# Three waits at stage boundaries removed, and 8 to 14 unread identity products on TensorE at the end of four stages

## The reference, cut to what matters

```python
x = x + jnp.tanh(g_xattn[0]) * _L0_xattn_ref(_layernorm(x), ctx, ctx, Wq, bq, Wk, bk, Wv, bv, interference, amp, Wo, bo)
x = x + jnp.tanh(g_ffn[0])   * _L0_ffn_ref(_layernorm(x), W, bias, A, Bf, coeffs, scales)       # dense + low rank
x = x + jnp.tanh(g_xattn[1]) * _L1_xattn_ref(_layernorm(x), ctx, Wq, bq, Wk, bk, Wv, bv, Wo, bo) # window of 16 keys
x = x + jnp.tanh(g_ffn[1])   * _L1_ffn_ref(_layernorm(x), weight, bias, centroids, assignments)  # clusters select
```

## Time and profile before

| | |
|---|---|
| three runs | 2049.05, 2052.22, 2054.82 us (median 2052.22) |
| the profiled execution's own time | 2051.24 us |
| its span, first to last instruction | 2049.1 us |
| PE busy | 1948.1 us, 95% of the span |
| mean granted TensorE clock | 0.980 |
| DVE, ACT, POOL busy | 52%, 33%, 18% |
| DMA | 328.62 MB, mean 160 GB/s |

### The profile page before, as it was taken

One profiled execution on the slowest core, in us unless ns is written; L12 is line 12 of the kernel. 1 busy time (PEld: TensorE's weight loads), 2 busy tenths in 40 slices (PEclk: granted clock), 3 DMA queues, 4 the chain that ended last, 5 costly groups with the idle time before them and its releaser, 6 DMA issues. The chain is left out here.

```text
span 2049.1 us, 50169 instructions
## 1 busy us (share of the span) xinstructions
PE 1948.1 (95%) x20126; PEld 1582.2 (77%) x20126; DVE 1072.4 (52%) x1868; ACT 681.4 (33%) x1152; POOL 360.1 (18%) x332
## 2 busy tenths in 40 slices
PE   7999889999997999999999899999689999999999
PEld 7999889999996777777777477777467777777887
DVE  5444241112114555555555465555578888874445
ACT  2222231111102344444434211111156666665121
POOL 0000000000001111111101210000256666651000
PEclk9999999999997899999999999999799999999999
DMA  5332335433348545544543434544664444433434
GB/s 200 124 123 103 145 106 184 169 122 137 116 163 300 204 167 215 203 174 190 226 185 115 161 113 185 184 184 164 198 188 149 140 131 142 148 113 114 150 134 147
DMA packets 149431, 328.62 MB, mean 160 GB/s; under 512 B 56433, under 2 KB 82673, under 8 KB 141105
## 3 DMA queue, kind: packets, MB, share of 16 engines
q1 hardware_dynamic: 147344, 326.04, 44.5%
q10 hardware_dynamic: 1952, 0.60, 0.1%
HBM read 200.25 MB, written 125.83 MB: 159 GB/s over the span
## 5 line engine op out<-in xcount | busy, mean ns | idle before, releaser
L1191 ACT ACTIVATE a_pt<-a_st_bank 128x1024 f32<-128x1024 f32 x128 | 131.3, 1026 | 266.3 <-PE a_st_bank L1239 266.3
L1528 POOL TENSOR_TENSOR a_sm<-a_sm,a_nmax 113x1024 f32<-113x1024 f32 x84 | 159.7, 1908 | 89.2 <-DVE a_nmax L1581 89.2
L1137 DVE TENSOR_REDUCE a_nmax<-a_s_bank 128x8 f32<-128x1024 f32 x124 | 151.7, 1223 | 20.6 <-PE a_s_bank L1227 14.0
L226 PE MATMUL q_qb<-q_xt_hi,wq_hi 128*128 128x256 f32 x512 | 146.2, 286 | 2.8 <-DVE wq_lo L168 2.8
L226 PE MATMUL kv_banks<-kv_ct_hi,wk_hi 128*128 128x256 f32 x512 | 146.0, 285 | 2.9 <-DVE wk_lo L168 2.9
L226 PE MATMUL kv_banks<-kv_ct_hi,wk_lo 128*128 128x256 f32 x512 | 145.5, 284 | 0.0
L226 PE MATMUL q_qb<-q_xt_lo,wq_hi 128*128 128x256 f32 x512 | 145.4, 284 | 0.0
L226 PE MATMUL q_qb<-q_xt_hi,wq_lo 128*128 128x256 f32 x512 | 145.4, 284 | 0.0
L226 PE MATMUL kv_banks<-kv_ct_lo,wk_hi 128*128 128x256 f32 x512 | 145.4, 284 | 0.0
L1821 PE MATMUL a_s_bank<-a_ks,a_qs 64*49 64x256 f32 x1344 | 95.5, 399 | 24.4 <-DMA a_ks<-k 11.8
L1575 DVE TENSOR_TENSOR a_sm<-a_s_bank,a_band 113x1024 f32<-113x1024 f32 x84 | 102.6, 1222 | 21.4 <-PE a_s_bank L1821 18.2
(11 more groups left out here) (228 smaller groups left out, 4595.2 us busy)
## 6 DMA issues: line engine op xcount, KB each, us to landing
k<-raw SPq DMA_DIRECT2D x32, 512.0 KB, 4.6
a_qs<-q SPq DMA_DIRECT2D x16, 1024.0 KB, 5.2
a_ks<-k SPq DMA_DIRECT2D x16, 1024.0 KB, 7.1
a_vraw<-v SPq DMA_DIRECT2D x32, 304.0 KB
q_xin<-in_x SPq DMA_DIRECT2D x16, 512.0 KB, 5.6
q<-q_out_lo SPq DMA_DIRECT2D x16, 512.0 KB, 4.1
q<-q_out_hi SPq DMA_DIRECT2D x16, 512.0 KB, 4.8
kv_cin<-in_ctxT SPq DMA_DIRECT2D x8, 1024.0 KB, 5.5
```

Of the source, the lines that this page charges most:

```text
L226: m = pe.matmul(out, a(x, c), b(y, c), start=(i + j == 0), stop=(len(terms) * j + i == n - 1))
L1137: dve.tensor_reduce(to, scores[:].rearrange("p b (h x) -> p b h x", h=4), X, ALU.max, negate=True).then_inc(maxed, 1)
L1191: act.activation(pt[:, s % 2], st_bank[:].rearrange("p b (h x) -> p (b h) x", h=4), ACT.Exp).then_inc(expd, 1)
L1528: pool.tensor_tensor(sm[live, k], sm[live, k], nmax[live, k, :].unsqueeze(2).to_broadcast([LIVE, 16, KEYS]), ALU.add).then_inc(shifted, 1)
```

## The change

Four parts, all at the boundaries.

1. A helper `keep_clock` multiplies the identity by itself n times into a PSUM tile that nobody reads: 14 products at the end of project_q, project_kv and ffn0_project1, 8 at the end of attention0. In project_kv PE waits first for the last key output (`klo`).
2. project_kv no longer loads `a_k_second`; `k_second` is no tile of its own any more, and attention0 loads the keys of slot 1 itself, as its third DMA.
3. In attention0 the loads of slot 2 wait for nothing new. Those of slot 3 now wait until ACT has written the first row of maxima (`rowed`).
4. The first queries and keys of layer 1 and the mask are loaded in the last turn of ffn0_project1, into SBUF that the low-rank factors have left. POOL zeroes that place in ffn0_project1, so half of the zeroing at the start of attend1_select_ffn1 falls away. The feed-forward weights' high part `f1_hi` is split over two places to make room.

```diff
+def keep_clock(pe, e, bank, n):
+    for _ in range(n):
+        pe.matmul(bank, e.ident[:], e.ident[:], start=True, stop=True)
...
@@ project_q, PE, end
+            keep_clock(pe, e, tb[:, 0, 0:P], 14)
...
@@ project_kv, SP
-            def last_keys(s):
-                if s == 1:
-                    sp.wait_ge(k_out, 160 * G + START)
-                    unit_keys(1)
...
-            staggered(sp, G, 2, [(2, load), (None, first_units), (None, output_weights), (0, store_k), (None, last_keys), (0, store_v)],
+            staggered(sp, G, 2, [(2, load), (None, first_units), (None, output_weights), (0, store_k), (0, store_v)],
...
@@ project_kv, PE, end
+            pe.wait_ge(klo, done(NC * G - 1))
+            keep_clock(pe, e, kb[:, 0, 0:P], 14)
...
@@ ffn0_project1, SP
+            def first_operands(s):
+                if s == 1:
+                    sp.wait_ge(e.op_zero, 2)
+                    for j in range(2):
+                        sp.wait_ge(qk_out[j][0], 16 + START)
+                    sp.dma_start(e.qs_first[:, 0:D], e.q1[0]).then_inc(e.op_in, 16)
+                    for c in range(4):
+                        sp.dma_start(e.ks_first[c:P:4, c, PADL:PADL + D], e.k1[0][c:P:4, :]).then_inc(e.op_in, 16)
+                    sp.dma_start(e.band[:], e.i["band"]).then_inc(e.op_in, 16)
+
+            steps = [(None, first_operands), (4, load_x), (1, load_ctx), (0, store_qk(1, e.k1)), (1, store_x2),
...
@@ ffn0_project1, POOL, after the first three roots
+            pool.wait_ge(w.lr, NC)
+            pool.memset(e.ks_first[:], 0.0).then_inc(e.op_zero, 1)
+            pool.memset(e.qs_first[:, D:DPAD], 0.0).then_inc(e.op_zero, 1)
...
@@ attention0, SP
+            sp.wait_ge(e.k_out, 160 * (B // 2 - 1) + START)
...
-                if s % G or filling(u):
+                if s % G or filling(u) and u == 0:
                     return
...
-                if isinstance(u, int) and u == NU:
-                    sp.wait_ge(shift_in[0], 16)
+                if isinstance(u, int) and u == NU + G:
+                    sp.wait_ge(rowed, 1)
                 sp.wait_ge(st_done, done(u - 13))
...
@@ attention0, PE, end
+            keep_clock(pe, e, s_bank[:, 0, 0:P], 8)
...
@@ attend1_select_ffn1
-            sp.wait_ge(pads[0], 2)
...
+                    if isinstance(t, int) and t == 0:
+                        continue
...
-                if s == -16:
-                    sp.dma_start(band[:], e.i["band"]).then_inc(const, 16)
...
-            pool.memset(ks[:, 0, 2:4], 0.0).then_inc(pads[0], 1)
-            pool.memset(qs[:, :, D:DPAD], 0.0).then_inc(pads[3], 1)
+            pool.memset(qs1[:, D:DPAD], 0.0).then_inc(pads[3], 1)
...
-            dve.memset(ks[:, 0, 0:2], 0.0).then_inc(pads[0], 1)
```

More of the change, by code:

```diff
@@ L46 @@
 DPAD = 1048
+HOLD = 5312
 NCL = 64
@@ L751, in ffn0_project1 @@
         sb, ps, sem = scope(nc, ctx)
+        sb("f0_hold", [P, HOLD - 4 * D])
         ln1 = Norm(nc, ctx, "fln"); ln2 = Norm(nc, ctx, "pln")
@@ L771, in ffn0_project1 @@
         qk_out = [[later(e, nc, f"p1_{c}_out{k}") for k in range(2)] for c in "qk"]
+        e.op_zero = later(e, nc, "a_op_zero"); e.op_in = later(e, nc, "a_op_in")
         e.f0_out = [*x_out, *v_out, *qk_out[0], *qk_out[1]]
@@ L1003, in attention0 @@
         qs = e.q_first + [sb(f"a0_qs{k}", [P, pairs, P], F32R) for k in range(2, 4)]
-        ks = e.k_first + [sb(f"a0_ks{k}", [P, pairs, P], F32R) for k in range(2, 4)]
+        ks = e.k_first + [sb(f"a0_ks{k}", [P, pairs, P], F32R) for k in range(1, 4)]
         vpad = sb("a0_vpad", [P, 2, 64, HP])
@@ L1340, in attend1_select_ffn1 @@
         x_bank = ps("se_x_bank", [P, 2, 512])
-        const = sem("a_const"); zeroed = sem("a_zeroed"); pads = [sem(f"a_pads{k}") for k in range(4)]; ps_zeroed = sem("a_ps_zeroed"); go = sem("a_go")
+        zeroed = sem("a_zeroed"); pads = [sem(f"a_pads{k}") for k in range(4)]; ps_zeroed = sem("a_ps_zeroed"); go = sem("a_go")
         qk_in = [sem(f"a_qk_in{k}") for k in range(2)]
@@ L1740, in weights_hi @@
             def weights_hi(r):
-                act.activation(f1_hi[:, r, :], raw[:, r, :], ACT.Copy).then_inc(whi, 1)
+                act.activation(f1_hi(r), raw[:, r, :], ACT.Copy).then_inc(whi, 1)
             def rows_hi(t, s, i):
@@ L1810, in score @@
                 for g in range(LOOP):
-                    if first(g) == s:
-                        pe.wait_ge(qk_in[g % 2], 80 * (2 * i + g // 2 + 1))
+                    if first(g) == s and LOOP * i + g == 0:
+                        pe.wait_ge(e.op_in, 96)
+                    elif first(g) == s:
+                        pe.wait_ge(qk_in[g % 2], 80 * (2 * i + g // 2 + g % 2))
                 pe.wait_ge(added, free(u, 1))
@@ L1892, in chunk @@
             def chunk(t, s, h, c):
-                for x, w in ((f1_hi_t, f1_hi), (f1_hi_t, f1_lo), (f1_lo_t, f1_hi)):
-                    m = pe.matmul(s_bank[:, h, :], x[s % 2][:, c, :], w[:, c, h * 512:(h + 1) * 512],
-                                  start=c == 0 and w is f1_hi and x is f1_hi_t, stop=c == NC - 1 and x is f1_lo_t)
+                for n, (x, w) in enumerate(((f1_hi_t, f1_hi(c)), (f1_hi_t, f1_lo[:, c, :]), (f1_lo_t, f1_hi(c)))):
+                    m = pe.matmul(s_bank[:, h, :], x[s % 2][:, c, :], w[:, h * 512:(h + 1) * 512],
+                                  start=c == 0 and n == 0, stop=c == NC - 1 and n == 2)
                 if c == NC - 1:
```

56 lines of the change are left out of this document (31 added, 25 removed).

## The result

The changed kernel is slower: 2055.19 us against 2050.82 us before, medians of 20 runs each. The two medians are 4.4 us apart. The ratio over all runs is 1.0025, with a 95% interval of 1.0015 to 1.0035, and that is +5.1 us on 2050.82, small but clear of noise. The forecast was -5.1 us.

A forecast was written before the change was run, and what follows sets the result against it. Bound: PE's work at full clock plus what the boundaries cost. Gains 0.5 + 2.3 + 0 + 2.3 = 5.1 us took the profiled 2051.24 to 2046.1, forecast 2047.0 as a median; range 2040 to 2052.7, main case 2043.5 to 2050.

The forecast's parts named there:

- The price of the products: Identity products at the four boundaries: 0.22 us each, fourteen 3.1 us, eight 1.8 us, free unless PE is last.
- project_q to project_kv: First boundary: products fit into PE's 6.13 us barrier wait at cost 0; clock gain 0.5 us, bounds 0 and 1.8.
- The kept clock: First boundary: if the clock outlives the remaining 3.0 us gap, folding at full speed gains 1.8 us.
- project_kv to attention0, the barrier: Second boundary: barrier 0.85 us earlier; products take back 1.4 us of the 2.2 us the removed wait frees.
- Slot 1's keys, and slot 2: Opening of attention0: keys take 6.9 us, unit 4 waits 2.0 us, unit 8 starts earlier; gain 2.3 us.
- The chain from unit 4 to the end of the first values: Opening of attention0: takes 8.2 us as before, so from 651.9 it ends at 660.1, when unit 8 starts.
- The sign of a clock that is kept: Opening of attention0: PE coming in at full clock and staying there would show the forecast wrong; kept-clock rival 15%, 2040.3 us.
- attention0 to ffn0_project1: Third boundary: eight products fit into 4.25 us of waiting, cost 0; DVE waits for the bias load, gain 0.
- ffn0_project1: In this stage: POOL's 3.55 us zeroing falls into 7.39 us of POOL waiting; six DMA issues, about 4 us, hidden.
- ffn0_project1 to attend1_select_ffn1: Last boundary: PE scores 4.9 us earlier, but the mask waits behind DVE's zeroing; gain 2.3 us.
- the bound of 3.7: Last boundary: upper bound of the gain, 3.7 us, if the products hold nothing up; lower bound 0.9 us.
- Slot 1's keys are late: Rival, opening of attention0: keys land at 654.7, that part gives -0.5 us and the kernel takes 2050; 20%.

The follow-up runs named there:

- e16: e10 plus the 14 identity products at the end of project_q alone; 2044.86 us (5 runs), ratio 0.9965 to the kernel before.
- e10: Kernel before plus preload with early zeroing and old tile remainders; attention0 loads slot 1's keys first, slot 2 still waits for the row; 2043.48 us, ratio 0.9971.
- e5: Changed kernel with POOL zeroing the new tiles ahead of its root for the third tile instead of behind it; 2052.01 us, ratio 1.0005 to the kernel before.
- e8: Changed kernel with last-stage tiles shifted 256 to 768 bytes, to the kernel before's remainders to 512 bytes; one run, 2049.70 us.
- e15: Changed kernel with the edits of e5 and e8 together; 2048.11 us, ratio 0.9992 to the kernel before.
- e3: Kernel before with only the changed key loads of attention0 (parts 2 and 3), no products or preload; 2052.03 us, ratio 1.0009.
- e6: Kernel before with only the changed kernel's SBUF places in ffn0_project1 and attend1_select_ffn1, loads and zeroing as before; 2052.87 us, ratio 1.0010.
- e14: Kernel before with f1_hi alone shifted by 128 bytes; matmul distance 0.2290 us; single times of the four shift runs 2051.47 to 2056.99 us.
- e2: Kernel before with only the identity products at the four places (and the wait at klo) added; 2050.99 us, ratio 0.9999.
- e1: Changed kernel without its identity products at all four places (and without the wait at klo); 2053.61 us, ratio 1.0013 to the kernel before.
- e7: Changed kernel with slot 3's loads waiting until the first row of maxima has landed, not until ACT has written it; 2053.27 us, ratio 1.0016.

## Why the prediction was wrong

**The price of the products** was right: 28 records took 3.29 us, 3.1 forecast; eight fit into the third boundary, which stayed 4.24 us.

**project_q to project_kv**: gain 0.5 forecast. The times of e16 and e10 can't tell it, the traces can. From project_q's last product to project_kv's first projection it is 25.2 us in the mean of the seven traces with the products and 25.6 in the eleven without: gain 0.4. The kept clock isn't worth the 1.8 us that I gave it. In the trace after, the clock fell at 241.0, just behind PE's start, and 3.4 us of folding ran at half clock instead of 3.6. In e16 it did not fall at all here, yet the projection started only 0.75 us earlier than in e10: a faster PE meets the weight loads.

```profile
243.65 7.38 PE L155 MATMUL kv_banks<-fold,raw 128*128 128x128 f32 x64 [3.01 <-PEq L79]
251.22 5.62 PE L155 MATMUL kv_banks<-fold,raw 128*128 128x128 f32 x48 [0.19 <-DMA raw<-in_Wk]
257.56 2.05 PE L155 MATMUL kv_banks<-fold,raw 128*128 128x128 f32 x16 [0.71 <-DMA raw<-in_Wk]
```

(e16, is the same place before.)

**project_kv to attention0, the barrier**: 0.85 us earlier forecast, 0.91 measured. The products took back 1.9 us there instead of 1.4. The agreement is in part luck: the old start scatters from 5.4 to 6.9 us, and against its mean of 6.1 the gain is 1.7.

**Slot 1's keys, and slot 2**: gain 2.3 forecast, loss measured: the part was 57.0 to 58.5 us long in the four kernels with these loads and products (after, e5, e8, e15), mean 57.5, against 55.99 in the trace before, +1.5, and against the mean of 56.4, +1.1. Two sizes were off. The keys took 8.5 us behind two other loads (7.1 when they go out first, in e10), not 6.9, so unit 4 waited 4.43 us and not 2.0. And in "The chain from unit 4 to the end of the first values", 8.2 us, I carried over 2.1 us for the row of maxima, which had had the DMA engines to itself behind the old wait; with 2 to 4 MB under way it took 4.8, and 7.9 in e3, while PE waited 3.06 and 6.12 us. I had named what SP's old wait held back, but not whom it protected. e10, which brings that protection back, has about the 2.3 us that I forecast for the change. The sign of a clock that is kept did not come true: PE came in at full clock but lost it 2.9 us later, and the clock came back 34.1 us after it had fallen before, 30.7 us after.

**attention0 to ffn0_project1**: 0 forecast, 0 measured.

**ffn0_project1**: the step that failed most. The forecast put POOL's zeroing at nothing, since "it falls into 7.39 us in which POOL waits", and looked at POOL's queue alone. The zeroing ran beside DVE's `f_rows` and held it for 3.3 us; the stage took 3.1 us more, and e5 takes them back by moving the zeroing ahead of the root. The Trainium skill (SBUF — State Buffer, Who interferes with whom) says that VectorE and GpSimd share a pair of SBUF ports, that an instruction of VectorE in a two-port mode, which a tensor_scalar can be, contends with GpSimd, and that whichever comes second waits for the whole of the other. By this rule the zeroing was a cost, and the trace agrees: 0.81 us becomes 4.12 beside a zeroing of 3.60 that began 0.08 us earlier. The six DMA issues were hidden, as forecast: e5 has them and its stage is as long as that of e6, which has not, 308.6 us.

**ffn0_project1 to attend1_select_ffn1**: gain 2.3 forecast, 2.9 measured. Right in mechanism: the score came 5 us earlier and the mask still waited for the zeroing. Without the products the gain would be 4.2, above the bound of 3.7.

**What no step priced**: that `f1_hi` was "split over two places to make room". I read it as free. It cost 3.0 us by the distance between matmuls, in the changed kernel and in e6, and e8 gives it back.

Of my 5.1 us, then: opening +1.1 to +1.5 instead of -2.3, zeroing +3.1, places +3.0, last boundary -2.9, first boundary -0.4, in sum +3.9 to +4.3, where +5.1 (3.1 to 7.2) were measured. The rival "Slot 1's keys are late" was true in kind: they landed 8.5 us after their issue, within its bounds, and the row of maxima, which no rival named, cost about as much again. The range ended at its worst case, with no room for edits that I had costed at nothing.

## What to carry to other kernels

Work that is moved onto an idle engine needs two covers: that engine's idle time, and that nothing critical on the neighbour with which it shares ports runs beside it; put a GpSimd zeroing where VectorE does other kinds of work. Before a wait in front of large loads is removed, look for the small transfer that it lets through, and keep the small one first. A new layout in SBUF is an edit with a price: compare the distance from matmul to matmul before and after, even in a stage that the change doesn't mean to touch.

## What the runs showed of the hardware

Matmuls of 128x128 by 128x512 in float32, in turns with a high and a low part of operand and weights, start 0.227 us apart when all their tiles start at the same remainder to 256 bytes, whichever of the two that were tried it is (0 or 128), 0.229 when `f1_hi` is off by 128, and 0.231 in the changed layout. At full clock that is 1% to 2% of the time of these matmuls, with no wait shown anywhere; only the mean of one (389 against 393 ns) and the count in a window tell. In e14 only the matmuls that read the shifted tile are slow. Whether the size of the tiles matters, and what the other operand's place does for itself, was not tried.

The unread products ahead of the four barriers raised the mean granted clock of a run from 0.980 to 0.983, and the kernel was no faster (e2). A small DMA of ACT took 2.1 us when no large load was under way and 4.3 to 7.9 us beside 2 to 4 MB of SP's loads (after, e1, e3, e5, e7, e8, e15). A zeroing on POOL held one kind of DVE's operations (f_rows, 0.81 to 4.12 us) and left another as it was (f_lo, 1.22 us each).
